# Attention and adaLN block on one core: q and k of two heads and two batches made of seven block products instead of eight

## The reference, cut to what matters

```python
h = _layernorm(x) * (1 + ca) + sa
q = _mxfp4_matmul(h, wq_codes, wq_scales) + bq      # 2048 x 256 @ 256 x 2048; k and v alike
scores = jnp.einsum('bqhd,bkhd->bhqk', q, k) / jnp.sqrt(jnp.float32(HEAD_DIM))
attn = jax.nn.softmax(scores, axis=-1)
out = jnp.einsum('bhqk,bkhd->bqhd', attn, v).reshape(B, S, NUM_HEADS * HEAD_DIM)
x = x + ga * (_mxfp4_matmul(out, wo_codes, wo_scales) + bo)
h = _layernorm(x) * (1 + cb) + sb
x = x + gb * ffn(h)                                  # dense 256 x 256, top 2 of 8 adapters of rank 16
```

## Time and profile before

| what | value |
|---|---|
| time, median of 3 runs | 774.33 us (774.06 to 774.34) |
| span of the profiled execution | 771.9 us |
| the profiled execution's own time | not reported apart from its span; the median of the runs is 2.4 us above the span |
| PE busy | 766.2 us, 99% of the span |
| DVE / ACT / POOL busy | 84% / 67% / 62% |
| PE's share of the chain that ended last | 98% |
| granted PE clock | full in all 40 slices |
| HBM traffic | 30 GB/s over the span |

### The profile page before, as it was taken

How to read it: one execution, slowest core, us unless ns; L and a number is a source line. 1 busy time by engine, 2 the same in 40 slices (tenths; PEclk the granted TensorE clock), 3 DMA queues, 4 the chain that set the end, 5 groups by cost and what they waited for, 6 DMA issues and landing times.

```text
span 771.9 us, 14746 instructions
## 1 busy us (share of the span) xinstructions
PE 766.2 (99%) x4212; PEld 667.1 (86%) x4212; DVE 650.9 (84%) x1259; ACT 520.4 (67%) x1133; POOL 481.1 (62%) x452
## 2 busy tenths in 40 slices
PE   8999999999999999999999999999999999999998
PEld 7888888888888888888888888888888888888897
DVE  7899889888888888888888888888888888879876
ACT  4788666766667676767676667676767676766841
POOL 5488566647655575547656675656657476789632
PEclk9999999999999999999999999999999999999999
DMA  8354465544454345544455434443455334433202
GB/s 260 96 153 123 98 146 151 143 101 100 125 145 125 95 98 139 138 111 99 114 142 134 99 93 134 133 129 92 105 137 152 96 92 108 113 87 86 55 1 110
DMA packets 71118, 89.92 MB, mean 116 GB/s; under 512 B 19409, under 2 KB 36522, under 8 KB 71086
## 3 DMA queue, kind: packets, MB, share of 16 engines
q1 hardware_dynamic: 52368, 73.21, 37.0%
q10 hardware_dynamic: 18718, 16.32, 7.3%
HBM read 21.30 MB, written 2.11 MB: 30 GB/s over the span
## 4 chain that ended last, share of the span: by engine, by line
PE 98%; DVE 1%; ACT 0%; issue 0%; POOL 0%; POOLq 0%
PE score L1202 10%; PE score L1203 10%; PE score L1204 9%; PE qv L1202 8%; PE qv L1204 8%; PE qv L1203 8%; PE o L1202 7%; PE o L1203 7%; PE o L1204 7%; PE ky L1202 4%; PE ky L1203 4%; PE ky L1204 4%; PE y L1202 2%; PE y L1204 2%; PE y L1203 2%; PE score L1408 1%
## 5 line engine op out<-in xcount | busy, mean ns | idle before, releaser
L432 POOL TENSOR_TENSOR pT_lo<-pT,pT_hi 128x512 fp32r<-128x512 f32 x248 | 314.6, 1305 | 238.0 <-ACT pT_hi L614 237.9
L708 ACT ACTIVATE prob<-score,neg_max 128x512 f32<-128x512 f32 x256 | 172.7, 688 | 78.5 <-DVE neg_max L1027 78.3
L1027 DVE TENSOR_REDUCE neg_max<-score 128x1 f32<-128x512 f32 x256 | 160.0, 682 | 1.3 <-PE score L1204 1.2
L1040 DVE STREAM_TRANSPOSE pB<-prob 128x512 f32<-128x512 f32 x252 | 156.7, 678 | 0.0
L614 ACT ACTIVATE pT_hi<-pT 128x512 fp32r<-128x512 f32 x248 | 135.3, 620 | 0.1
L1202 PE MATMUL score<-k_hi,q_hi 128*128 128x512 f32 x256 | 101.2, 395 | 0.2 <-DVE q_lo L934 0.2
L1203 PE MATMUL score<-k_lo,q_hi 128*128 128x512 f32 x256 | 100.3, 392 | 0.0
L1204 PE MATMUL score<-k_hi,q_lo 128*128 128x512 f32 x256 | 99.6, 389 | 0.0
L1202 PE MATMUL o<-pT_hi,v_hi 128*128 128x512 f32 x248 | 96.6, 389 | 0.0
L1204 PE MATMUL o<-pT_hi,v_lo 128*128 128x512 f32 x248 | 96.5, 389 | 0.0
L1203 PE MATMUL o<-pT_lo,v_hi 128*128 128x512 f32 x248 | 96.5, 389 | 0.0
(11 more groups left out here) (302 smaller groups left out, 1835.4 us busy)
## 6 DMA issues: line engine op xcount, KB each, us to landing
pT<-pB SPq DMA_DIRECT2D x1008, 64.0 KB, 2.0
out_dram<-x_nat SPq DMA_DIRECT2D x8, 256.0 KB, 2.3
stage<-in_L_attn_wv_codes_dram ACTq DMA_DIRECT2D x7, 256.0 KB
stage<-in_L_attn_wv_scales_dram ACTq DMA_DIRECT2D x14, 128.0 KB
stage<-in_L_attn_wq_codes_dram ACTq DMA_DIRECT2D x7, 256.0 KB
...
```

What stands on the lines that cost most here:

```text
L432: pool.tensor_tensor(split(pT_lo, kt), turned(par, kt), split(pT_hi, kt).bitcast(f32), ALU.subtract).then_inc(p_lo_ok, 1)
L708: act.activation(prob[:, i], score_ps[i][:, :], ACT.Exp, bias=neg_max[:, i:i + 1], accum_out=row_sum[:, s % 2, i:i + 1]).then_inc(exp_ok, 1)
L1027: dve.tensor_reduce(neg_max[:, i:i + 1], score_ps[i][:, :], AX.X, ALU.max, negate=True).then_inc(max_ok, 1)
L1040: dve.transpose(pB[:, s % 2, :, i].rearrange("p g k q -> p k g q"), prob[:, i].rearrange("p (k g q) -> p k g q", k=QT, g=G)).then_inc(pB_o ...
```

## The change

From pair 1 on, q of a pair of heads for a pair of batches is one 2x2 block product: two blocks of input features by two heads for the weights, two blocks of input features by two batches for the inputs. Before, each of the four results took two block products, eight in all. Now seven products of sums and differences give the same four results (Strassen's scheme in Winograd's form), for q and for k, each product again three matmuls of 512 columns. One such cycle spans four steps and starts in the step before them.

- PE: in the step before a cycle products 1 and 2 (in two score banks, `first_ps`), in its step 0 products 6, 7 and 4, in step 1 product 5, in step 2 product 3, each for q and k. In step 3 the next cycle begins.
- The heads within a pair now follow the order 0, 1, 1, 0 (`HEADS`).
- ACT copies running sums out of PSUM (`first_copied`, `sum_kept`), and makes the high parts of two of the four results from SBUF (`mixed_high`). DVE adds the kept sum and the bias (`mixed_sum`) where it made a low part before, and POOL makes the low parts of these two (`mixed_low`).
- POOL sums the weight blocks (`block_sums`) and splits five groups of them. The sums of the inputs are made once, in pair 0 (`input_mix`), and stay in SBUF for the whole kernel.
- Room for this: the input sums take the place of `x_nat`, which is loaded again in the last pair (four loads on the SP queue), `hT32` goes, and `pB` has one half instead of two. `pT32` keeps its two.
- v is projected into the bank of the fourth score tile, ahead of the output projection; the fourth score tile waits for v's low part.
- `three`, the exponentials, the transposes' shape and the 16 DMAs of a step stay.

```diff
-        pB = sb("pB", [P, 2, G, QT, QT, 32])
+        pB = sb("pB", [P, G, QT, QT, 32])
...
+        HEADS = (0, 1, 1, 0, 0, 1, 1, 0)
...
+        v_ps = score_ps[3]
+        y_ps = [o_ps[1], score_ps[2]]
+        y_end = [score_ps[3], o_ps[0]]
+        end_ps = [*score_ps[0:2], score_ps[3], qv_ps]
+        f_banks = [*score_ps[0:2], *y_ps, score_ps[3], score_ps[0], o_ps[0], ky_ps]
+        mix_ps = dict(q=qv_ps, k=ky_ps)
+        first_ps = dict(q=score_ps[0], k=score_ps[1])
...
                     for a in range(G):
                         for g in range(G):
                             sp.dma_start(flat(pT32[32 * g:32 * (g + 1), par, a]),
-                                         flat(pB[32 * a:32 * (a + 1), par, g])).then_inc(p_land[par], 16)
+                                         flat(pB[32 * a:32 * (a + 1), g])).then_inc(p_land[par], 16)
+                    if last and s == 1:
+                        sp.wait_ge(product_mm["k"], products(5, cycle(p, 0) + 1))
+                        for b in range(B):
+                            load_x(b)
...
+            def block_sums(m, p):
+
+                w = w32[m]
+                a11, a12, a21, a22 = w[:, 0, 0:HD], w[:, 1, 0:HD], w[:, 0, HD:PW], w[:, 1, HD:PW]
+                pool.wait_ge(w_prod[m], p + 1)
+                pool.tensor_tensor(s_sum(m, 1), a21, a22, ALU.add).then_inc(s_summed, 1)
+                pool.tensor_tensor(s_sum(m, 3), a11, a21, ALU.subtract).then_inc(s_summed, 1)
+                pool.wait_ge(s_summed, summed(m, p, 2))
+                pool.tensor_tensor(s_sum(m, 2), s_sum(m, 1), a11, ALU.subtract).then_inc(s_summed, 1)
+                pool.wait_ge(s_summed, summed(m, p, 3))
+                pool.tensor_tensor(s_sum(m, 4), a12, s_sum(m, 2), ALU.subtract).then_inc(s_summed, 1)
...
+            def mixed_low(m, src, count):
+
+                pool.wait_ge(mix_hi, mixes(m, count))
+                hi, lo = {"q": (q_hi, q_lo), "k": (k_hi, k_lo)}[m]
+                pool.tensor_tensor(lo[:, :], src[m], hi[:, :].bitcast(f32), ALU.subtract).then_inc(mix_ok, 1)
...
+            def first_copied(m, count):
+
+                act.wait_ge(product_mm[m], products(1, count))
+                act.activation(mix_ps[m][:, :], first_ps[m][:, :], ACT.Copy).then_inc(kept_ok[m], 1)
+
+            def sum_kept(m, i, to, count):
+                act.wait_ge(product_mm[m], products(i, count))
+                act.activation(to[m], mix_ps[m][:, :], ACT.Copy).then_inc(kept_ok[m], 1)
+
+            def mixed_high(m, src, count):
+                act.wait_ge(mix_sum, mixes(m, count))
+                act.activation({"q": q_hi, "k": k_hi}[m][:, :], src[m], ACT.Copy).then_inc(mix_hi, 1)
...
+                    if t == 0:
+                        exps(n, s, range(3))
+                        for m in "qk":
+                            sum_kept(m, 6, u2, now)
+                        exps(n, s, range(3, QT))
+                        for m in "qk":
+                            sum_kept(m, 7, u3, now)
+                        o_high(n - 1)
+                        q_high(SPP + 2 * now, 1)
+                        k_high(SPP + 2 * now, 1)
+                        prob_and_v(p, s)
+                    elif t == 3:
+                        exps(n, s, range(QT))
+                        first_cycle_step(p, s)
+                    else:
+                        exps(n, s, range(QT))
+                        for m in "qk":
+                            mixed_high(m, u3 if t == 1 else u2, 2 * now - 2 + t)
+                        o_high(n - 1)
...
+            def mixed_sum(m, src, i, what, count, head):
+
+                dve.wait_ge(product_mm[m], products(i, count))
+                dve.wait_ge(kept_ok[m], kept(what, count))
+                dve.scalar_tensor_tensor(out=src[m], in0=mix_ps[m][:, :], scalar=bias[:, "qk".index(m), head], in1=src[m],
+                                         op0=ALU.add, op1=ALU.add).then_inc(mix_sum, 1)
...
+            def turn(p, s, i):
+                n = SPP * p + s
+                early = isinstance(p, int) and p == 0
+                dve.wait_ge(exp_ok, QT * n + i + 1)
+                if i == 0 and not (early and s == 0):
+                    dve.wait_ge(p_land[(s - 1) % 2], landed(p, s - 1))
+                if i == QT - 1 and not (early and s < 2):
+                    dve.wait_ge(p_lo_ok, QT * (n - 1))
+                dve.transpose(pB[:, :, i].rearrange("p g k q -> p k g q"),
+                              prob[:, i].rearrange("p (k g q) -> p k g q", k=QT, g=G)).then_inc(pB_ok, 1)
...
-                    def turn(i):
-                        dve.wait_ge(exp_ok, QT * n + i + 1)
-                        if i == 0 and not early:
-                            dve.wait_ge(p_land[s % 2], landed(p, s - 2))
-                        if i == QT - 1 and not early:
-                            dve.wait_ge(p_lo_ok, QT * (n - 1))
-                        dve.transpose(pB[:, s % 2, :, i].rearrange("p g k q -> p k g q"),
-                                      prob[:, i].rearrange("p (k g q) -> p k g q", k=QT, g=G)).then_inc(pB_ok, 1)
-
-                    if not early and not end:
...
+            def pair(p, last=False):
+                for s in range(SPP):
+                    n = SPP * p + s
+                    t, now = s % 4, cycle(p, s // 4) + 1
+                    nxt = (s + 1) % SPP
+                    for i in range(QT):
+                        maximum(n, i)
...
+                    if t == 1:
+                        for m in "qk":
+                            mixed_sum(m, u3, 5, "u3", now, head_at(p, s + 1))
+                    elif t == 2:
+                        for m in "qk":
+                            mixed_sum(m, u2, 3, "u2", now, head_at(p, s + 1))
+                    for i in range(QT):
+                        turn(p, s, i)
+                    inverse(n, s)
+                    if s == 0:
+                        bv_through_wo(p)
+                    o_low(n - 1)
+                    if t == 0:
+                        q_low(SPP + 2 * now, head_at(p, s + 1))
+                        k_low(SPP + 2 * now, head_at(p, s + 1))
...
+            def product(dst, m, i, b, first):
+
+                j, pb = "qk".index(m), b // 2
+                a = {1: (0, slice(0, HD)), 2: (1, slice(0, HD)), 4: (1, slice(HD, PW)), 5: (0, slice(HD, PW))}
+                if i in a:
+                    weights = tuple(w[m][:, a[i][0], a[i][1]] for w in (w_hi, w_lo))
+                else:
+                    weights = tuple(w[:, j, {6: 0, 7: 1, 3: 2}[i]] for w in (s_hi, s_lo))
+                if i in (1, 2, 3):
+                    rows = (slice(None), 0 if i == 1 else 1, tokens(b + 1 if i == 3 else b))
+                    inputs = hT_hi[rows], hT_lo[rows]
+                else:
+                    inputs = t_hi(pb, {4: 4, 5: 1, 6: 2, 7: 3}[i]), t_lo(pb, {4: 4, 5: 1, 6: 2, 7: 3}[i])
+                return three(dst[:, :], weights, inputs, first, True, not first)
...
+                for i in range(QT):
...
+                        pe.wait_ge(exp_ok, QT * (n - 1) + i + 1)
+                        if i == 2 and not (first and s < 3):
+                            pe.wait_ge(y_ok, QT * (n - 2))
+                        if i == 3:
+                            pe.wait_ge(v_lo_ok, n + 1)
+                    cut = (slice(None), slice(i * P, (i + 1) * P))
+                    three(score_ps[i][:, :], (q_hi[cut], q_lo[cut]), (k_hi[:, :], k_lo[:, :]),
+                          True, True).then_inc(s_mm, 1)
...
+            def next_v(p, s):
+                n, nxt = SPP * p + s, (s + 1) % SPP
+                if s == SPP - 1:
+                    pe.wait_ge(w_ok["v"], p + 2)
+                pe.wait_ge(exp_ok, QT * (n + 1))
+                project_v(batch_of(nxt), nxt % 2).then_inc(v_mm, 1)
...
+            def first_outputs(p, s):
+
+                n, made = SPP * p + s, cycle(p, s // 4) + 2
+                b, j = batch_of((s + 1) % SPP), HEADS[(s - 2) % SPP]
+                weighted_ready(p, s)
+                weighted(n - 2, batch_of(s - 2) % 2, j, range(2))
+                for i, m in enumerate("qk"):
+                    if s == SPP - 1:
+                        pe.wait_ge(w_ok[m], parts_of(m, p + 1) + 1)
+                    pe.wait_ge(exp_ok, QT * n + i + 1)
+                    product(first_ps[m], m, 1, b, True).then_inc(product_mm[m], 1)
+                weighted(n - 2, batch_of(s - 2) % 2, j, range(2, QT))
+                for m, done in (("q", q_mm), ("k", k_mm)):
+                    pe.wait_ge(kept_ok[m], kept("copy", made))
+                    product(first_ps[m], m, 2, b, False).then_inc(done, 1)
+                next_v(p, s)
+                out_projection(p, s)
...
+                    if t == 0:
+                        for m in "qk":
+                            pe.wait_ge(kept_ok[m], kept("copy", now))
+                            pe.wait_ge(w_ok[m], parts_of(m, p) + 2)
```

(21 more changed lines are left out.)

909 lines of the change are left out of this document (557 added, 352 removed).

## The result

The changed kernel takes 968.29 us (median of 4 runs, 967.10 to 971.89) against 774.34 for the kernel before on the same chip (4 runs, 774.06 to 775.28): a ratio of 1.2508, 95% interval 1.2483 to 1.2533. The profiled execution took 967.1 us with a span of 965.3.

What follows compares the result with a forecast made beforehand. The closed ring of transposes, issues and landing was taken as the bound: start 25.4, 62 rings of 14.1 us (874.2), irregular steps 16, loads 1, end 56.5, a span of 973.1; with 2.4 above the span, 975 us, range 945 to 1010.

Steps and rivals of the forecast that it cites:

- The ring: Each step: transposes, 16 serial issues, landing, then next transposes, closed by the single `pB` half; 14.1 us, chance 0.85.
- the release: DVE's start after the last landing, within each step; taken as 0.05 us, bounds 0 and 0.5 us.
- Irregular steps: Longer issue groups and landings, mostly in the first sixteen and last six steps; 16 us added, bounds 0 and 30.
- The loads: Four extra `x_nat` loads on SP between steps 57 and 58, in SP's wait; 1 us, bounds 0 to 6.
- What the ring hides: In each step, extra DVE, ACT and POOL work, PE's longest step of 12.4 us and stalls stay under 14.1 us.
- The walk: DVE's work followed from the end of a step's transposes: done before T + 8, landing T + 11.6, 3.6 us to spare.
- The end: From step 62's transposes to the finish: 56.5 us instead of 58.5, as PE finishes everything else before the landing; bounds 54 and 60.
- Waits: In the trace after: DVE waits some 280 us for landings, SP about 4 us per step, PE idle near 200 us.
- a sign that I was wrong: A falling granted clock of PE in the trace after was listed among the signs against the prediction.
- third rival: PE's clock falls in its new waits: 975 to 1005 us, near 1410 if throughout; chance of leaving the range 0.05.
- first rival: Issues get cheaper, PE stays the bound and saves 19.1 us of matmuls: 755 us; chance 0.04 together with the hand-overs.
- the second: Ring doesn't bind; new hand-overs before the output projection cost 28 x 0.4 = 11 us: about 766 us; shared chance 0.04.

Runs made afterwards that it cites:

- experiment 1: Kernel before, all eight products and both `pB` halves; only the wait ahead of a step's first transpose changed, to the landing of the step before: 970.97 us.
- Experiments 4 and 5: Changed kernel from the second pair on: with 12 instead of 16 DMAs into `pT` per step, 847.36 us; with sixteen DMAs of half the bytes, 960.83 us.
- experiment 6: Changed kernel with spare matmuls ahead of each output projection of the second to seventh pair: 983.78 us with sixteen, 968.63 us with six.
- in place: Changed kernel, exponentials written into a two-half tile and transposed where they lie, so no step's first transpose waits for a landing: 790.43 us.
- experiment 10: In-place kernel with moved waits and reordered first pair; b_v through w_o moved to a pair's second step, last pair's batch 0 statistics one step later: 795.30 us.
- 7: In-place kernel with two waits moved: output projection starts on `o_hi` alone, DVE asks for zeroed `y_acc` rows only at first use: 786.13 us.

## Why the prediction was right, point by point

975 us was predicted, 968.29 measured, and the mechanism is the one named; experiment 1 shows it alone. The nearness owes a little to luck: against the span of the profiled execution, rings, irregular steps and loads came out 11.4 us under my 891.2, start and end 3.6 us over.

- The ring. Predicted 14.1 us a step. Steady steps took 13.93 to 14.2: transposes 2.49, 0.03 to the first issue, mostly 9.42 and up to 9.6 between the first and the last, 1.98 landing, 0.02 or 0.09 for DVE's release. The 0.636 us between issues of the earlier trace rows is 0.628 in most steps, which makes most of the difference between 14.1 and 14.0. For the release I had taken 0.05; its upper bound of 0.5 us is not half the distance of two issues, as I wrote, but over three quarters of it. Experiments 4 and 5 confirm the form of the sum, the number of issues times a fixed time.
- Irregular steps. 16 us predicted. 62 rings took 879.8 us (from 25.96, where 25.4 was predicted, to 905.76), 11.8 more than 62 at 14.0. From first to last issue the 63 groups came to 7.7 us more than 63 times 9.42, where in the kernel before it is 14.7; the rest lies mainly in late landings and in steps 8 and 61 (below).
- The loads. Their four issues, 843.25 to 845.27, fell into SP's wait, and step 58 took 14.05 us. Step 59 took 15.37, with a late landing, but in experiment 1, which has no such loads, steps 58 and 59 took 15.24 and 14.73; no run tells the term of 1 us from nothing.
- What the ring hides. PE, ACT, POOL and the new stalls stayed under it, as worked out, but for two steps. In steps 8 and 61 (14.5 and 15.2 us) DVE waited for no landing; in step 61 it made the residual (1.9 us) and the statistics of batch 0 (2.0 us) ahead of the maxima. Elsewhere the 0.28 us that DVE waited at 493.72, 0.25 to 0.36 in one step of each later pair, shows how close it came: I had said 3.6 us to spare, and the step with b_v through w_o, followed by the sums, used nearly all of it. The walk left out b_v through w_o (2.3 us of DVE in one step of a pair) and the lower clock of PE.
- The end. 56.5 us predicted, from 58.5 before (771.9 less 713.3 is 58.6), 59.5 measured, inside my bounds but for the wrong reason. I had said that PE would have finished all else when the last DMAs landed. The last issue began at 915.2, so the landing came at about 917.2, but DVE began the low parts only at 920.37, for it was late itself: it waited 1.81 us for PE's output projection, made the residual, the maxima and the statistics of batch 1 (2.3, 2.5 and 2.5 us), and waited 1.54 us for o's high part. In the ring of experiment 1 the end took 58.7 us and before 58.6: the ring gives nothing back there.
- Waits. DVE's for the landings came to 210 us, not 280: it does more per step than I had reckoned. SP's for the transposes came to 258 us, 4.1 per step, where I had said 4. PE was idle for 144.6 us (965.3 less 820.7), not near 200, since it ran slower behind its waits.
- The clock. I had named a fall of the granted clock as a sign that I was wrong, and it fell, to 0.93 over the span. So the third rival's condition came true, without its price: the time is under its 975 to 1005 us, and a higher clock did not shorten it (experiment 6). The sign was badly chosen, for it says nothing against the ring.
- The gain. For an open ring the first rival took 19.1 us off for the matmuls, and the second gave 766 us with the hand-overs. Its hand-over term was of the right size: 28 x 0.4 = 11 us expected, 1.64 us a pair measured, 11.5 in seven. What I had not priced is that the first pair pays for the operands (+18.2 us up to step 10, a part through DVE, more through POOL's backlog behind that pair) and that the last pair is longer (+4.2). With the ring open the change gives 790, not 766. This had no weight in 975, as the ring covered it.

The rule of the Trainium skill (DMA: Bandwidth & Descriptors, "Issuing engines are not separate DMA queues") that initiating a DMA is usually small beside the DMA does not hold for these DMAs: the issue is 0.59 us of the 2.0 from its start to the landing, sixteen in a row take 9.5, and it is the same 591 ns at half the bytes.

What stays open: the 4 us of the last pair. They lie in step 61, 18.4 us in place against 12.8 before, while the other steps of that pair are 1.4 us shorter in all. Taking the statistics of batch 0 out of it made it 1.9 us shorter (experiment 10, against 7); for the rest I have no cause.
